# The shared expert's gate-up product one slot later, and rank matmuls merged from 13 to 7

## The reference, cut to what matters

```
x = x + attn(layernorm(x))          # scan: state = dA * state + dB ; y = sum(state * C) + D * u ; y * silu(z) @ out_w
h = layernorm(x)
probs = softmax(h @ gate_w);  top 2 of 8 experts, weights normalized
out = sum over the two of w_e * (silu(h @ w_gate[e]) * (h @ w_up[e])) @ w_down[e]
so  = (silu(h @ sw_gate) * (h @ sw_up)) @ sw_down          # the shared expert, width 352
out = out + sigmoid(h @ shared_gate_w) * so
x = x + out
```

## Time and profile before

| | us |
|---|---|
| time of the profiled execution | 2948.53 |
| span of its trace | 2946.7 |
| median of the 3 timed runs | 2950.19 |
| TensorE busy | 2601.8 (88%) |
| VectorE busy | 2246.7 (76%) |
| GpSimd busy | 2235.6 (76%) |
| ScalarE busy | 2030.5 (69%) |

### The profile page before, as it was taken

How to read it: one execution, slowest core, us unless ns; L and a number is a source line. 1 busy time by engine, 2 the same in 40 slices (tenths; PEclk the granted TensorE clock), 3 DMA queues, 4 the chain that set the end, 5 groups by cost and what they waited for, 6 DMA issues and landing times.

```text
span 2946.7 us, 49244 instructions
## 1 busy us (share of the span) xinstructions
PE 2601.8 (88%) x15616; PEld 2291.2 (78%) x15616; DVE 2246.7 (76%) x4890; ACT 2030.5 (69%) x4675; POOL 2235.6 (76%) x1354
## 2 busy tenths in 40 slices
PE   7888888888888888888888888888887599999998
PEld 4777877878787778877877778787776488888887
DVE  2989999999998999899989989998998233333332
ACT  3878888888888888888888888888875133333332
POOL 2989998989898989889998989898986033333333
PEclk9889999999999989999999999899987699999999
DMA  4222222222222222222222222222221288888886
GB/s 171 83 77 76 77 77 83 77 76 86 92 83 80 78 84 85 77 88 79 77 76 82 79 76 82 94 85 80 73 81 35 95 199 202 201 202 201 202 200 152
DMA packets 138184, 309.67 MB, mean 105 GB/s; under 512 B 15040, under 2 KB 79680, under 8 KB 137792
## 3 DMA queue, kind: packets, MB, share of 16 engines
q1 hardware_dynamic: 110848, 270.03, 29.5%
q0 software_dynamic: 27072, 36.46, 6.2%
HBM read 258.42 MB, written 48.01 MB: 104 GB/s over the span
## 4 chain that ended last, share of the span: by engine, by line
PE 52%; DVE 22%; ACT 10%; issue 8%; POOL 2%; DMA 1%; SPq 0%; DVEq 0%; ACTq 0%; POOLq 0%
PE bank L662 13%; DVE bank L1242 10%; PE bank L680 9%; PE bank L563 7%; PE bank L600 6%; DVE room L1242 4%; PE bank L552 4%; DVE room L1251 4%; ACT bank L809 3%; ACT room L793 3%; PE bank L530 2%; PE bank L580 2%; PE bank L616 2%; PE bank L570 2%; PE bank L644 2%
## 5 line engine op out<-in xcount | busy, mean ns | idle before, releaser
L1031 POOL TENSOR_TENSOR room<-dtu,b_all 128x1024 f32<-128x1024 f32 x512 | 1202.6, 2370 | 26.4 <-DVE dtu L1419 13.5
L809 ACT ACTIVATE bank<-room,eps_col 128x512 f32<-128x512 f32 x1024 | 693.9, 683 | 282.6 <-DVE carry L1256 202.4
L793 ACT ACTIVATE room<-room,neg_a 128x256 f32<-128x256 f32 x2048 | 867.9, 497 | 0.8 <-DVE room L1208 0.8
L600 PE MATMUL bank<-ident,room 128*128 128x128 f32 x4096 | 589.8, 295 | 236.8 <-DVE room L1251 215.7
L600 PEld LDWEIGHTS bank<-ident,room 128*128 128x128 f32 x4096 | 513.1, 153 | 302.1 <-DVE room L1251 232.3
L1020 POOL TENSOR_TENSOR room<-room,c_all 128x1024 f32<-128x1024 f32 x224 | 532.1, 2375 | 122.9 <-DVE bank L1242 87.7
L1242 DVE TENSOR_TENSOR_SCAN bank<-room,carry,bank 128x256 f32<-128x256 f32 x864 | 580.5, 735 | 48.6 <-ACT bank L809 47.7
L1156 POOL DMA_INDIRECT out<-room,ids x144 | 223.8, 1554 | 409.8 <-DMA out<-room,ids 217.9
L1321 DVE SCALAR_TENSOR_TENSOR hid<-hid,bank 128x256 f32<-128x256 f32 (+1 forms) x312 | 131.1, 420 | 453.8 <-ACT hid L904 453.7
L1242 DVE TENSOR_TENSOR_SCAN room<-room,carry,bank 128x256 f32<-128x256 f32 x672 | 446.1, 728 | 1.1 <-DVE hot L1292 0.5
L552 PE MATMUL bank<-xnT,w_conv 128*128 128x256 f32 x3072 | 404.2, 288 | 7.0 <-ACT xnT L832 5.5
(11 more groups left out here) (150 smaller groups left out, 3095.4 us busy)
## 6 DMA issues: line engine op xcount, KB each, us to landing
b_all<-b_scratch SPq DMA_DIRECT2D x128, 512.0 KB, 4.0
c_all<-b_scratch SPq DMA_DIRECT2D x128, 512.0 KB, 5.5
room<-in_wgu SPq DMA_DIRECT2D x72, 704.0 KB, 5.9
room<-in_wd SPq DMA_DIRECT2D x72, 384.0 KB, 3.6
room<-x_by_expert SPq DMA_DIRECT2D x72, 260.0 KB, 2.9
x_in<-in_x SPq DMA_DIRECT2D x32, 256.0 KB, 6.1
x<-in_x SPq DMA_DIRECT2D x32, 256.0 KB, 2.7
out<-x SPq DMA_DIRECT2D x32, 256.0 KB, 4.2
```

The costliest lines, as they stand in the source:

```text
L600: last = mm(tr_bank[k][:, b * P:(b + 1) * P], v[n % VRING][:, b, k * P:(k + 1) * P], ident[:, :], is_transpose=True, start=False, stop=(n ...
L793: last = af(da[n % RING][:, b, :], dt[c.par][:, b, :], ACT.Exp, scale=neg_a[:, b, n:n + 1])
L809: af(v_slot(c, n, h)[:, :], v[n % VRING][:, 2 * h:2 * h + 2, :].rearrange("p b t -> p (b t)"), ACT.Identity, bias=eps_col[:, 0:1]).then_in ...
L1031: nc.gpsimd.tensor_tensor(out=v[n % VRING][:, :, :], in0=dtu[:, :, :], in1=row, op=ALU.mult) \
```

## The change

Three things are edited. VectorE's `gated` gets a list of its own, `GATED_SLOT`, one slot behind the old one for each unit. Unit 2's matmuls go from slot 13 to 14 and its tanh from slot 14 to 15. `post_rank` issues seven wider matmuls instead of thirteen narrow ones: one spreads `base` over all three groups of 8 columns by a broadcast operand, two (one per pick) multiply both token blocks with `upper` at once, and four (pick x block) add a block's counts to every later group. The sums are the same.

```diff
-GU_SLOT, GATE_SLOT = [11, 12, 13], [12, 13, 14]
+GU_SLOT, GATE_SLOT, GATED_SLOT = [11, 12, 14], [12, 13, 15], [13, 14, 15]
...
-                for k in range(NT + 1):
-                    place = o_bank[:, k * EXPERTS:(k + 1) * EXPERTS]
-                    mm(place, ones[0:1, :], base[0:1, :], start=True, stop=False)
-                    for b in range(min(k + 1, NT)):
-                        for n in range(PICKS):
-                            last = mm(place, (upper if b == k else ones)[:, :], hot[:, n, b, :], start=False,
-                                      stop=(b == min(k, NT - 1) and n == PICKS - 1))
+                mm(o_bank[:, 0:(NT + 1) * EXPERTS], ones[0:1, :],
+                   base[0:1, :].unsqueeze(1).to_broadcast([1, NT + 1, EXPERTS]), start=True, stop=False,
+                   skip_group_check=True)
+                for n in range(PICKS):
+                    mm(o_bank[:, 0:NT * EXPERTS], upper[:, :], hot[:, n, :, :], start=False, stop=False,
+                       skip_group_check=True)
+                for n in range(PICKS):
+                    for b in range(NT):
+                        later = NT - b
+                        last = mm(o_bank[:, (b + 1) * EXPERTS:(NT + 1) * EXPERTS], ones[:, :],
+                                  hot[:, n, b, :].unsqueeze(1).to_broadcast([P, later, EXPERTS]), start=False,
+                                  stop=(n == PICKS - 1 and b == NT - 1), skip_group_check=True)
...
-                            for u in units_of(slot, GATE_SLOT):
+                            for u in units_of(slot, GATED_SLOT):
                                 gated(post, u, False)
```

## The result

The changed kernel takes 2905.11 us (median of 4 runs, 2903.36 to 2906.05) against 2949.4 us before (with a fourth run beside the three above): a ratio of 0.9849, 95% interval 0.9836 to 0.9862. The forecast was 2906 us. One execution of `slots_gated_only` (2947.49 us) and one of the kernel before (8431.14 us) ran in a slow state and stand in no median and no ratio.

A forecast was written before the change was run, and what follows sets the result against it. No engine was full; VectorE, the busiest, waited on other engines' chains. From 2948.5 us, gains of 28.9 + 14.5 - 3.4 + 2.8 = 42.8 us gave 2905.7, said as 2906; own range 2893 to 2917, 8 in 10: 2872 to 2940.

The forecast's parts named there:

- The tanh waits: VectorE's loop waits for ScalarE's shared-expert tanh vanish with products a slot later: 28.9 us, 0.96 a chunk.
- Unit 2's product behind the last state's: TensorE's down-projection chain starts 0.84 us earlier relative to VectorE, cutting output-projection waits: 14.5 us over 30 chunks.
- The down projection's new wait: TensorE's wait for unit 2's product: none at half clock, 0.6 us at full, still 1.2 us ahead of before.
- the wait for the output projection: VectorE's wait for TensorE's output projection in the loop should fall from 19.6 to about 5 us.
- GpSimd as the cap: GpSimd's chain limits the gain in two of four chunks, by 0.40 and 0.08 us: 3.4 us over 30.
- Unit 2's matmuls: Moving them a slot later on TensorE costs 0, at worst 0.5 us that its idle time takes up.
- The rank matmuls: TensorE saves 1.56 us a chunk, worth about nothing in the loop (0 to 0.32), 2.8 us in the last chunk.
- everything moves: Rival: TensorE keeps its high clock; output-projection waits and half the bank waits go too: 2864 us; chance 0.13.

The follow-up runs named there:

- slots_gated_only: Against the kernel before: only VectorE's three shared-expert products one slot later, thirteen rank matmuls kept; 2898.04 us, ratio 0.9835.
- slots_u2_ahead: Against the kernel before: VectorE's products of units 0 and 1 one slot later, unit 2 and the thirteen rank matmuls unchanged; 2907.41 us, ratio 0.9854.
- slots_only: Against the kernel before: the change's three slot lists, with the thirteen rank matmuls kept ("the slots alone"); 2894.37 us, ratio 0.9816.
- gated_only: Against the changed kernel: unit 2's matmuls and tanh back in slots 13 and 14, products still one slot later; 2899.24 us, ratio 0.983.
- with the constants early as well: Changed kernel with GpSimd's second-layernorm constants ahead of its slot 5 product and three filling matmuls before the B/C projection's wait; 2875.5 us, ratio 0.9742.

## Why the prediction came out right, step by step

**The tanh waits (28.9 us): mechanism right, size too small.** The wait is gone (0.5 us left), and unit 2 has none. But what the waits cost was more than what the trace listed as idle. Before, the two slots from scan to scan with a late product took 5.22 us each; now they take 4.66 and 4.67, so a listed wait of 0.45 us cost 0.55. Most back-to-back VectorE instructions here start 0.07 to 0.09 us before the one ahead has ended, and a wait loses that overlap too. The Trainium skill ("VectorE: DVE Perf Modes", section "Two Vector instructions with no wait between them") says that a held instruction starts only when every earlier Vector instruction has finished, and gives no figure for the others. By that rule the instructions that start 0.07 to 0.09 us early in these traces aren't held. Over slots 12 to 15 that makes 1.14 us a chunk in the chunk of the earlier trace rows (from 18.30 to 17.16 us with the slots alone, from the first scan of slot 12 to that of the next slot 0), some 34 us over 30 chunks instead of 28.9, if every chunk is like that one.

**Unit 2's product behind the last state's (14.5 us, 11 after the cap): sign and mechanism right, size not settled.** `slots_u2_ahead` against `slots_only` gives 13 us, with two things changed; against `slots_gated_only`, with one, it gives 9 us, not clear of the spread. The down projection's new wait is there, 0.38 us in the row of L680 above (the one at 1212.01), since the transposes ahead of it ran fast; the prediction had priced that case as harmless. In the changed kernel only part shows: the wait for the output projection stayed at 8.5 us instead of the expected 5, because in one chunk of four it is still near 1 us (with the slots alone 0.27).

**GpSimd as the cap: right in size and place.** The periods of the four chunks fell by 2.5, 0.7, 2.5 and 1.0 us with the slots alone. By the prediction's own terms, in the order of the earlier trace rows, they would fall by 1.74, 0.76, 1.89 and 0.99: the two that it capped came out nearly exactly, the two others were undersized, in part by the first item and by taking TensorE's gain as 0.84 us at most, where the greater part of the waits of 0.97 and 1.47 us went. That the cap is the reason in the other two is argued from this fit; no run took the cap away alone. In the changed kernel the mean period fell by 1.17 us, less than the 1.3 to 1.4 that was forecast, and from 69.09 us, not from the 68.5 that the prediction took from three chunks.

**Unit 2's matmuls (0): not contradicted**, within the spread of `gated_only` and `slots_gated_only`, whose medians differ by 6 and 4 us, in opposite directions, from the kernels with the matmuls a slot later.

**The rank matmuls (2.8 us, all in the last chunk): the step that failed.** The last chunk's gain is 2.9 us, as worked out, and with the slots of before the loop gains nothing. But "in the loop this is worth about nothing" had bounds of 0 to 0.32 us a chunk, and beside the moved slots of the change it costs 11 us in all and 14.6 us in the 28 chunks (67.92 against 67.40 us a period). The bound excluded a loss on the ground that TensorE had idle time there. It had: and in the changed kernel longer idle time stood ahead of the B/C projection, and the clock fell behind it in work that VectorE waits for (11 of the 14.6 us). Why the wait for the output projection is longer in one chunk of four too (5 us) isn't known, and with the two other slot lists the merged rank is no loss. The rival "everything moves" had seen the fast down projection (2.83 us) as a gain of 2.3 us; where it occurs, it was no gain.

The Trainium skill's rule on weight loads ("TensorE: Matmul & The Clock Gate", section "LDWEIGHTS (loading the stationary operand)") would have given an estimated 1.3 us for the last chunk; the trace has 2.9, and the measurement decides: with the clock at its lower level a pass took 0.23 us, not the 107 ns of a load.

**What else moved.** The pass of the last scan lost three tanh waits (1.91, 0.53 and 0.52 us in the trace of before). They lay outside the window of the earlier trace rows, and the prediction didn't count them. With the slots alone the last interval fell from 48.85 to 44.34 us, 4.5 of the 15 us by which the slots were undersized.

So the slots were forecast at 40 us of gain and brought 55; the rank was forecast at a gain of 3 us and cost 11 beside the slots. The sums, 43 and 44, agree.

What stays open: why the merged rank makes the down projection run fast, above all in that one chunk of each four. Padding the rank group and filling the following pause both left it fast in some chunks (10 and 6 of 28, against 11 in the changed kernel). That the place of the clock's fall behind the thirteen narrow matmuls decides where the later falls lie is a guess that no run isolates.

## What to carry to other kernels

In a loop of in-order engines, put a consumer a slot behind its producer on another engine where the producer waits for a release by that same consumer; and put work that nobody else needs behind what another engine's chain starts from. Count a removed stall at its slot's length, not at its listed idle time. Work taken off an engine that isn't the bottleneck is not always free: check where the idle time goes. Here matmuls on the path that stood behind a TensorE pause of over 2.6 us ran in part at the lower clock in 25 of 37 cases, and a few matmuls of no use in that pause gained 5 to 6 us, at the edge of the spread, or, with the constants early as well, left no such case. And try a change beside the neighbours that it will have: the same merged rank gained 10 us alone, lost 11 with one slot list and made no clear difference with two others.

## What the runs showed of the hardware that was not expected

The stretch from the B/C to the dt projection takes 11.16 us or 12.6 to 12.8, and nothing between, in all fourteen traces: a fall of the clock behind the pause ahead of it either is there or isn't. Even at equal pauses it is not certain: in the changed kernel six pauses of 3.7 us were followed by one and a seventh of 3.69 wasn't.

Behind the thirteen matmuls of 8 columns (3.4 us), the next z product took over 1.7 us from its start to the next matmul in 14 to 22 of 28 chunks in every kernel that has them; behind the seven of 8 to 24 columns (1.7 us) it took 1.46 to 1.55 us in every chunk of every kernel, unless they were padded with six narrow ones (slow in 20 of 28). Whether the width of the matmuls, their number or the time that the group takes makes the difference, no run separates. Matmuls of 8, 16 or 24 columns all took 0.12 to 0.13 us a pass at full clock.
